# Ends of the expert stages: second expert weighted on ScalarE, plain sums by chunk, and the next normalisation's statistics on VectorE

## The reference, cut to what matters

```python
for layer in range(4):
    xn = layernorm(x)                   # (x - mean) / sqrt(var + 1e-5)
    x = x + attention(xn) + ffn(xn)
# ffn of layers 1 and 2: the two best of eight experts, for each token
top2_w, top2_idx = top_k(softmax(logits(xn)), 2)   # weights, renormalised
x = x + top2_w[0] * expert[top2_idx[0]](xn) + top2_w[1] * expert[top2_idx[1]](xn)
```

## Time and profile before

| | |
|---|---|
| time, median of 3 runs | 1666.32 us (1662.14 to 1670.17) |
| the profiled execution | 1663.76 us |
| its span, first to last instruction | 1661.5 us |
| mean granted TensorE clock | 0.964 of full |
| busy: PE / PEld / DVE / ACT / POOL | 88% / 62% / 65% / 55% / 40% |
| end of layer 1's experts to start of layer 2's attention, from the first sum | 1002.97 to 1025.40 us |
| end of layer 2's experts to start of `ssm_prepare_stage`, from the first sum | 1322.43 to 1344.99 us |

### The profile page before, as it was taken

The page is one execution under the profiler, slowest core; times in us unless marked ns, Lnnn a source line. Parts: engine busy times, 40 slices in busy tenths (PEclk is TensorE's granted clock), DMA queues, the critical chain, the costliest instruction groups (busy, mean ns, idle before and its releaser), DMA issues. The chain is left out here.

```text
span 1661.5 us, 30953 instructions
## 1 busy us (share of the span) xinstructions
PE 1470.2 (88%) x10541; PEld 1027.0 (62%) x10541; DVE 1079.1 (65%) x2724; ACT 920.5 (55%) x2444; POOL 658.3 (40%) x863
## 2 busy tenths in 40 slices
PE   7999999889989998999999895889889686999976
PEld 5667666666666665778787663555557533555643
DVE  5588888875666654555444346777523387899964
ACT  3578888555555563544544341334444258878945
POOL 5799999611111001003220253314534303888820
PEclk8999999999999997999999997999999887999999
DMA  9000000000000003000000114000012212333300
GB/s 296 14 1 14 14 15 15 13 1 1 1 1 1 1 1 119 1 2 21 18 17 21 44 60 173 2 1 13 30 54 61 75 35 47 90 85 87 91 12 25
DMA packets 48433, 65.36 MB, mean 39 GB/s; under 512 B 7839, under 2 KB 34568, under 8 KB 47530
## 3 DMA queue, kind: packets, MB, share of 16 engines
q1 hardware_dynamic: 43738, 54.02, 11.0%
q0 software_dynamic: 4544, 9.38, 1.6%
HBM read 52.80 MB, written 15.77 MB: 41 GB/s over the span
## 5 line engine op out<-in xcount | busy, mean ns | idle before, releaser
L2412 POOL TENSOR_TENSOR weighted<-state,c_all 128x512 f32<-128x512 f32 x128 | 163.5, 1297 | 78.7 <-DVE state L2422 64.8
L798 ACT ACTIVATE probs<-psum_all,pair_shift 128x256 f32<-128x256 f32 x256 | 117.8, 472 | 77.2 <-POOL pair_shift L487 77.2
L2422 DVE TENSOR_TENSOR_SCAN state<-decay,psum_all 128x512 f32<-128x512 f32 x128 | 149.0, 1200 | 14.3 <-PE psum_all L2340 11.5
L971 DVE TENSOR_REDUCE pair_negmax<-psum_all 128x2 f32<-128x512 f32 (+1 forms) x192 | 114.9, 639 | 55.9 <-PE psum_all L657 55.3
L2049 POOL DMA_INDIRECT found<-values,dest x78 | 74.7, 957 | 156.1 <-ACT values L2042 138.8
L798 ACT ACTIVATE probs<-psum_all,pair_negmax 128x192 f32<-128x192 f32 (+1 forms) x192 | 81.5, 436 | 93.6 <-DVE pair_negmax L971 46.3
L500 POOL TENSOR_SCALAR probs<-probs,pair_recip 128x256 f32<-128x256 f32 x128 | 121.8, 959 | 5.1 <-DVE pair_recip L991 5.1
L809 ACT ACTIVATE probsT<-psum_all 128x512 f32<-128x512 f32 x224 | 122.5, 612 | 0.3 <-PE psum_all L672 0.3
L2350 PE MATMUL psum_all<-weighted,ident 128*128 128x512 f32 x256 | 121.7, 600 | 0.0
L672 PE MATMUL psum_all<-ident,probs 128*128 128x128 f32 x896 | 116.7, 273 | 0.1
L487 POOL TENSOR_SCALAR pair_shift<-pair_negmax,row_term 128x1 f32<-128x1 f32 x256 | 102.2, 418 | 34.9 <-DVE pair_negmax L971 34.9
(11 more groups left out here) (402 smaller groups left out, 3510.5 us busy)
## 6 DMA issues: line engine op xcount, KB each, us to landing
c_all<-c_rows SPq DMA_DIRECT2D x64, 256.0 KB, 3.3
slots<-slot_fill_dram SPq DMA_DIRECT2D x2, 2535.0 KB, 14.4
ring<-slots SPq DMA_DIRECT2D x18, 260.0 KB, 2.9
keys<-found SPq DMA_DIRECT2D x16, 256.0 KB, 4.6
scale_rows<-row_scales SPq DMA_DIRECT2D x8, 256.0 KB, 4.6
up<-up_dram SPq DMA_DIRECT2D x1, 2048.0 KB, 7.8
down<-down_dram SPq DMA_DIRECT2D x1, 2048.0 KB, 13.0
up<-up_dram SPq DMA_DIRECT2D x1, 1408.0 KB, 6.1
```

What stands on the lines that cost most here:

```text
L798: nc.scalar.activation(k.probs[:, 2 * (u % PAIR_BUF) + j, t, key_cols(u, t)], k.psum[score_bank(u, j)][:, score_cols(u, t)], ACT.Exp, bias ...
L971: nc.vector.reduce_max(k.pair_negmax[:, u % 2, SUB * j:SUB * (j + 1)], src, AXX, negate=True).then_inc(s.negmax_ready, 1)
L2412: nc.gpsimd.tensor_tensor(w.weighted[:, u % RING, :], w.state[:, u % RING, :], w.c_all[:, u // L3_DC % C_RING, :], ALU.mult)\
L2422: nc.vector.tensor_tensor_scan(w.state[:, u % RING, :], w.decay[:, u % L3_RING, :, :].rearrange("p b n -> p (b n)"), k.psum[u % PARTS_RING ...
```

## The change

Both `sparse_experts_stage` calls end differently, and the `layer_norm_stage` of layers 2 and 3 begins differently (`measured=True`, the default; layer 1's passes `measured=False` and stays as it was).

- ScalarE multiplies the second expert's rows by their weight, in place, four instructions a chunk as soon as the chunk has landed.
- VectorE adds the first expert as before (four instructions), and then the weighted second one for the whole chunk in one 128x512 addition.
- VectorE takes `bn_stats` of a chunk after the sums of the next chunk, `bn_aggr` one chunk later, then epsilon and reciprocal; ScalarE takes the square root. All of that is now in the expert stage; the normalisation stage starts with the 16 instructions that write `xn`.
- TensorE runs its five unread products in the expert stage, once the first expert of chunk 0 is added, and one more at the start of the normalisation stage in place of five.
- The expert stage has four more semaphores, which SP clears.

```diff
-def layer_norm_stage(nc, k, loads=(), router=None):
+def layer_norm_stage(nc, k, loads=(), router=None, measured=True):
...
-                for t in range(TILES):
-                    step.add(nc.vector.bn_stats(k.stats[:, t, :], k.x[:, t, :]))
...
-                nc.vector.reciprocal(k.rstd[:, :], k.rstd[:, :]).then_inc(s.moments_ready, 1)
-                dve.wait_ge(s.rstd_ready, 1)
+                if not measured:
+                    (the same lines)
...
-                keep_running(nc, k, 7, 5)
+                keep_running(nc, k, 7, 1 if measured else 5)
...
-                act.wait_ge(s.moments_ready, 1)
-                nc.scalar.activation(k.rstd[:, :], k.rstd[:, :], ACT.Sqrt).then_inc(s.rstd_ready, 1)
+                if not measured:
+                    (the same lines)
...  sparse_experts_stage, TensorE
+                pe.wait_ge(s.x_added, CT)
+                keep_running(nc, k, 0, 5)
...  ScalarE
+                for c in range(CHUNKS):
+                    act.wait_ge(fetched[c], 32)
+                    for t in range(CT * c, CT * (c + 1)):
+                        nc.scalar.activation(w.picked[:, 1, t, :], w.picked[:, 1, t, :], ACT.Copy, scale=k.gate_top[:, 1, t:t + 1]).then_inc(s.gated, 1)
+                act.wait_ge(s.moments_ready, 1)
+                nc.scalar.activation(k.rstd[:, :], k.rstd[:, :], ACT.Sqrt).then_inc(s.rstd_ready, 1)
...  VectorE
+                def add_chunk(c):
+                    dve.wait_ge(fetched[c], 32)
+                    for t in range(CT * c, CT * (c + 1)):
+                        nc.vector.scalar_tensor_tensor(k.x[:, t, :], w.picked[:, 0, t, :], k.gate_top[:, 0, t:t + 1], k.x[:, t, :], ALU.mult, ALU.add)\
+                            .then_inc(s.x_added, 1)
+                    dve.wait_ge(s.x_added, (CT + 1) * c + CT)
+                    dve.wait_ge(s.gated, CT * (c + 1))
+                    nc.vector.tensor_tensor(k.x[:, tiles_of(c), :], k.x[:, tiles_of(c), :], w.picked[:, 1, tiles_of(c), :], ALU.add).then_inc(s.x_added, 1)
...
                 for c in range(CHUNKS):
-                    dve.wait_ge(fetched[c], 32)
-                    for r in range(2):
...
+                    add_chunk(c)
+                    if c >= 2:
+                        step.wait()
+                        moments(c - 2)
+                    if c >= 1:
+                        statistics(c - 1)
+                step.wait()
+                moments(CHUNKS - 2)
+                statistics(CHUNKS - 1)
+                step.wait()
+                moments(CHUNKS - 1)
...  epsilon and reciprocal as they stood in layer_norm_stage
...
-        layer_norm_stage(nc, k, loads, router=(w.router[:, :], d["router1"]))
+        layer_norm_stage(nc, k, loads, router=(w.router[:, :], d["router1"]), measured=False)
```

More of the change, by code:

```diff
@@ L133, in _ @@
                 step = Steps(dve, s.dve_step)
-                for t in range(TILES):
-                    step.add(nc.vector.bn_stats(k.stats[:, t, :], k.x[:, t, :]))
[L136 to L141, removed]
-                nc.vector.reciprocal(k.rstd[:, :], k.rstd[:, :]).then_inc(s.moments_ready, 1)
-                dve.wait_ge(s.rstd_ready, 1)
+                if not measured:
+                    for t in range(TILES):
+                        step.add(nc.vector.bn_stats(k.stats[:, t, :], k.x[:, t, :]))
+                    step.wait()
+                    for t in range(TILES):
+                        step.add(nc.vector.bn_aggr(k.moments[:, t, :], k.stats[:, t, :]))
+                    step.wait()
+                    step.add(nc.vector.tensor_scalar(k.rstd[:, :], k.moments[:, :, 1], LN_EPS, None, ALU.add))
+                    step.wait()
+                    nc.vector.reciprocal(k.rstd[:, :], k.rstd[:, :]).then_inc(s.moments_ready, 1)
+                    dve.wait_ge(s.rstd_ready, 1)
                 for t in range(TILES):
@@ L1943, in sparse_experts_stage @@
                  "hidden_saved", "down_made", "y_saved", "flagged", "dest_ready", "stored_0", "stored_1", "stored_2", "stored_3",
-                 "fetched_0", "fetched_1", "fetched_2", "fetched_3", "x_added") as s:
+                 "fetched_0", "fetched_1", "fetched_2", "fetched_3", "gated", "x_added", "dve_step", "moments_ready", "rstd_ready") as s:
         loaded = (s.loaded_0, s.loaded_1, s.loaded_2)
@@ L2080, in _ @@
                         nc.vector.tensor_copy(w.hid_T[:, j % 2, 0:FC * P], k.psum[4 + j % 2][:, 0:FC * P]).then_inc(s.hidden_saved, 1)
-                for c in range(CHUNKS):
-                    dve.wait_ge(fetched[c], 32)
-                    for r in range(2):
[L2084 to L2088, removed]
+                step = Steps(dve, s.dve_step)
@@ new lines, in tiles_of @@
+                def tiles_of(c):
+                    return slice(CT * c, CT * (c + 1))
+                def add_chunk(c):
[6 more added lines that the diff above has]
+                    nc.vector.tensor_tensor(k.x[:, tiles_of(c), :], k.x[:, tiles_of(c), :], w.picked[:, 1, tiles_of(c), :], ALU.add).then_inc(s.x_added, 1)
@@ new lines, in statistics, with moments @@
+                def statistics(c):
+                    dve.wait_ge(s.x_added, (CT + 1) * (c + 1))
+                    for t in range(CT * c, CT * (c + 1)):
+                        step.add(nc.vector.bn_stats(k.stats[:, t, :], k.x[:, t, :]))
+                def moments(c):
+                    for t in range(CT * c, CT * (c + 1)):
+                        step.add(nc.vector.bn_aggr(k.moments[:, t, :], k.stats[:, t, :]))
+                for c in range(CHUNKS):
+                    add_chunk(c)
+                    if c >= 2:
+                        step.wait()
+                        moments(c - 2)
+                    if c >= 1:
+                        statistics(c - 1)
```

## The result

| | before | after |
|---|---|---|
| median of 6 runs each, same chip | 1665.16 us | 1675.92 us |
| ratio of the two (95% interval) | | 1.0057 (1.0038 to 1.0076) |
| the profiled execution, its span | 1663.76, 1661.5 us | 1666.78, 1665.0 us |
| VectorE busy / ScalarE busy | 1079.1 / 920.5 us | 1076.7 / 931.8 us |

The change made the kernel slower: +10.8 us between the medians, forecast +10.7. The ratio isn't the quotient of the medians (that would be 1.0065); turned into us it is +9.5. That measured and forecast agree says less than it seems: one of the two terms was too large and the other too small, as the experiments show. Also, the profiled execution of after is the fastest of its six (1666.8; the others 1674.3 to 1679.2), so its trace alone would explain 3 us and not 11.

The account below looks back on a forecast made before the run. Arithmetic was taken to end the first stretch, where TensorE's clock would be lost, and SP's 18 loads the second: +6.1 and +4.6 make +10.7 us, so 1674.5 profiled, median about 1676.5, range 1669 to 1682.

Parts of the forecast that it names:

- The meeting: End of both expert stages: the engines' meeting ahead of `xn` comes 11.3 us after chunk 1's landing.
- the row of L2556: Same-shape ScalarE instruction, 0.480 us with two per-partition operands; four take 1.67, an upper bound for ScalarE's products per chunk.
- the narrow sum saves 4 x 0.44 us: First stretch: saving named beside the -0.6 us for an earlier `xn`, partly offset by the root's hand-over and wide sums' waits.
- The second stretch, +4.6: Layer 2's experts into layer 3's normalisation: the later meeting delays SP's 18 loads, which set the stage's end; +4.6 us.
- 0.2 for four clears: Second stretch: four more semaphore clears delay SP's loads by at most 0.22 us, at least 0; 0.2 taken.
- -0.2 for TensorE's clock at the restart: Layer 3's start: TensorE restarts at low clock as before, rising up to 1 us sooner or later; -0.2 us.
- The first stretch, +6.1: Layer 1's experts into layer 2's attention: earlier `xn` -0.6, normalisation at low TensorE clock +4.7, attention start +2.0; chance 0.55.
- the 2.0: Layer 2's attention start at half clock: 16 products delay POOL's first addition by 1.4 us, plus a slower score group; +2.0.
- the score group that was to add half of 0.94: Layer 2's attention: score group takes 2.09 us instead of 1.15 at low clock, half of it before the first maximum.
- Rival C: SP's loads don't bind the second stretch and TensorE's clock isn't lost in the first: -1.2 us, 1665; chance 0.07.
- B: Rival: TensorE's clock comes back within layer 2's normalisation stage; +5.7 us in all, 1672; chance 0.27.
- D: Rival: low clock lasts into layer 2's attention score groups, +3.5 us more, so +14, 1680; chance 0.11.

Follow-up runs that it names:

- the split of the loads: ScalarE's queue issues 9 of layer 3's 18 loads: added to after, 1.0034 against before; added to before, 0.9992, -1.3 us.
- the ends measured alone: Kernel before with only one expert stage's end and the following normalisation changed, each twice: first end 1.0013 and 1.0027, second end 1.0039 and 1.0042.
- the sums alone: ScalarE's weighting and chunk sums kept in both expert stages, statistics and all five unread products back in the normalisation stage: 0.9982 against before, -3.0 us.
- the second measurement: The changed kernel, unaltered, measured once more against the kernel before: 1.0085 (1.0064 to 1.0106), +14.3 us, +11.3 between the medians.

## Why the prediction was right

**The meeting.** Right: `xn` starts 11.10 and 11.12 us after chunk 1's landing, forecast 11.3. Chunk 0 was hidden; ScalarE's four products took 1.28 us. Here the Trainium skill (ScalarE: Activation LUTs, section What ACT_TABLE_LOAD costs) had the number, an estimate of 1.27 by its rule for pointer operands, and the row of L2556 was the wrong neighbour. VectorE's wait for them was 0.24 us, not the 0.1 taken. In the first end `xn` had started 11.89 us after that landing. The prediction's side remark that the narrow sum saves 4 x 0.44 us counts chunk 0, which is hidden; the sum itself has three chunks.

**The second stretch, +4.6.** Right in mechanism, shown by the split of the loads: the traces give 4.5 from the landing of chunk 0 to the restart (means of 27.15 us in four traces, 22.6 in four with the old end). Its 0.2 for four clears measured 0.23, a little above the bound of 0.22. Its -0.2 for TensorE's clock at the restart is not shown: the first eight products took 6.67 us before and 5.86 after, and 5.06 to 6.62 in four other traces with layer 3's statistics behind the meeting and all loads on SP. Short in the time by 2 us that no trace places.

**The first stretch, +6.1.** The mechanism was right, and the price as well where it is paid: 12.78 us against a forecast of 12.5 from `xn` to the restart, and 32.0 - 26.0 = +6.0 to the first maximum against the profile of before. Behind the restart 1.75 of the 2.0 came, by the first 16 products (6.58 us for 3.69); the score group that was to add half of 0.94 ran at full clock (1.15 us). The step that failed is that this case was taken as what happens, against a baseline that never pays: of five traces the clock was back for all logits in one, back and lost again before the last 16 in one, and low throughout in three. And the baseline isn't the profile of before: in the three other traces with the old end the attention's first 16 products took 5.38 us, not the 3.69 of the earlier trace rows, so before often pays a part too. The term is +3.4, not +6.1.

**The sum.** +10.7 was 4.6 + 6.1; the ends measured alone are 6.8 + 3.4. The term of the first stretch was too large by 2.7 and that of the second too small by 2.2, so that the total came out right is partly luck. Rival C is refuted (the second end is longer in every trace of it), B is one trace of five, and D was not seen: the groups behind the first maximum ran at full clock.

**What was not foreseen**: that waits for ScalarE take 0.42 of the 1.05 us that the sums alone save at the first end and 0.24 at the second, that the clock can be lost with all five products beside the statistics too, and that the router's load would hold the logits (0.21 to 0.24 us, 0.80 with more products).

## What to carry to other kernels

Ask of a meeting of all engines what stands behind it on the engines that are not busy: work that is moved ahead of it makes their queues start later, and one of them may set the end. What unread products are worth is read from the granted clock under the work that they are for, in more than one trace: here five beside the statistics were worth 5.2 us, with the same five moved ahead of the meeting the first end cost 3.4 us on average, and twelve that ended behind VectorE's chain were waited for and gained nothing. Compare a trace with the spread of the timed runs before explaining its difference.

## What the hardware showed beyond that

Whether TensorE's clock comes back in a stretch of sparse work differs between executions of one kernel, here on two chips. In the trace of after it stood at 1.00 from 1021 to 1025 us; in that of the second measurement, with the same instructions, it stayed at 0.50 from 1017 to 1036 us:

```profile
1021.00:1025.00 4.00, 4.00 (x20) 3.70 (x19) 1.46 (x6) 1.43 (x3) 0.00 (x0) 0.50 0.59 181
```

And the kernel before took 1665 to 1666 us on two chips and 1678 to 1679 on three others, about as much as the largest effect of anything tried here.
